# Window attention and graph experts on one core: scores by quarters of the TensorE array, shift masks accumulated by matmul

## What is computed

```python
x = x + conv(layernorm(x))          # conv: two passes of window attention
t = x.reshape(32, 1024, 128)
t = t + ffn(layernorm(t))           # graph attention -> top 2 of 4 experts

def mhsa(x, w_qkv, b_qkv, w_o, b_o, mask):      # x: (images*16, 64, 128), 8 heads of 16
    q, k, v = split(x @ w_qkv + b_qkv)
    scores = einsum('bqhd,bkhd->bhqk', q, k) / sqrt(16)
    if mask is not None:            # second pass: -1e9 where the regions differ
        scores = scores + mask[:, None, :, :]
    attn = softmax(scores)
    return einsum('bhqk,bkhd->bqhd', attn, v) @ w_o + b_o
```

## Time and profile before

| what | us |
|---|---|
| time, median of 3 runs (lowest, highest) | 8315.46 (8314.64, 8325.83) |
| the profiled execution: its time, its span | 8316.28, 8314.6 |
| TensorE busy, matmuls | 4440.4 (53%) |
| VectorE busy | 5201.6 (63%) |
| ScalarE busy | 2132.3 (26%) |
| GpSimd busy | 4861.2 (58%) |
| last subtraction of a maximum (line 1104) ends | 2250.6 |

### The profile page before, as it was taken

How to read it: one execution, slowest core, us unless ns; L and a number is a source line. 1 busy time by engine, 2 the same in 40 slices (tenths; PEclk the granted TensorE clock), 3 DMA queues, 4 the chain that set the end, 5 groups by cost and what they waited for, 6 DMA issues and landing times. The chain is left out here.

```text
span 8314.6 us, 101072 instructions
## 1 busy us (share of the span) xinstructions
PE 4440.4 (53%) x29005; PEld 2290.4 (28%) x29005; DVE 5201.6 (63%) x15789; ACT 2132.3 (26%) x3826; POOL 4861.2 (58%) x5216
## 2 busy tenths in 40 slices
PE   5889888989834445344443535445353444535200
PEld 3555555555511212122121212212121121212100
DVE  9999888988945455454545545454554545445368
ACT  4666666666510101001010100101010010101034
POOL 2221111111167777777777777777777777777573
PEclk9999999999855656556565655656565565656555
DMA  1121111111111111111111111111111111111267
GB/s 47 45 54 49 48 48 49 49 49 47 54 40 43 32 43 32 32 43 32 43 32 43 32 32 43 32 43 32 37 37 32 43 32 42 32 35 39 79 194 254
DMA packets 537622, 419.47 MB, mean 50 GB/s; under 512 B 177554, under 2 KB 450498, under 8 KB 536642
## 3 DMA queue, kind: packets, MB, share of 16 engines
q1 hardware_dynamic: 323058, 323.88, 12.0%
q0 software_dynamic: 147552, 56.96, 7.0%
q10 hardware_dynamic: 66560, 33.56, 1.4%
HBM read 203.65 MB, written 176.72 MB: 46 GB/s over the span
## 5 line engine op out<-in xcount | busy, mean ns | idle before, releaser
L1321 POOL DMA_INDIRECT edge_G<-node_rows,edge_src x4352 | 4159.5, 956 | 1326.3 <-issue 1326.3
L1358 PE MATMUL edge_cbank<-edge_ohh,edge_ohl 128*128 128x256 bf16 x4096 | 1417.4, 395 | 2951.5 <-DVE edge_ohh L1491 2878.4
L1358 PEld LDWEIGHTS edge_cbank<-edge_ohh,edge_ohl 128*128 128x128 bf16 x4096 | 427.5, 104 | 3934.8 <-DVE edge_ohh L1491 3758.9
L1491 DVE TENSOR_SCALAR edge_ohh<-edge_iob,edge_dlf 128x256 bf16<-128x256 bf16 x4096 | 1193.6, 298 | 0.0
L561 POOL TENSOR_SCALAR attn_nw<-attn_mv 128x8 f32<-128x8 f32 x64 | 89.8, 1403 | 1814.4 <-DVE attn_mv L979 1814.3
L1490 DVE TENSOR_SCALAR edge_ohl<-edge_iob,edge_dlf 128x128 bf16<-128x128 bf16 x4096 | 1084.1, 265 | 14.8 <-DVE edge_dlf L1484 14.5
L1338 ACT ACTIVATE edge_hid<-edge_hbank,edge_b1c 128x512 f32<-128x512 f32 x512 | 351.6, 687 | 2498.2 <-PE edge_hbank L1365 2498.2
L1449 DVE COPY edge_O<-edge_O 128x24 f32<-128x24 f32 x64 | 12.4, 193 | 1533.2 <-DMA edge_G<-node_rows,edge_src 1533.2
L1501 DVE TENSOR_TENSOR edge_yo<-edge_ybank,edge_b2r 128x512 f32<-128x512 f32 x256 | 176.9, 691 | 946.9 <-PE edge_ybank L1374 946.9
L1341 ACT ACTIVATE edge_w<-edge_w 128x272 f32<-128x272 f32 x64 | 27.5, 429 | 2405.3 <-DVE edge_w L1463 2405.3
L859 PE MATMUL attn_score<-attn_km,attn_qT 128*64 128x512 f32 x2048 | 537.2, 639 | 176.0 <-DMA attn_km<-attn_kT 98.0
(11 more groups left out here) (239 smaller groups left out, 6424.5 us busy)
## 6 DMA issues: line engine op xcount, KB each, us to landing
edge_G<-node_rows,edge_src POOLq DMA_INDIRECT x4352, 2.4
expert_out<-edge_yo SPq DMA_DIRECT2D x64, 1024.0 KB
comb_ye<-expert_out SPq DMA_DIRECT2D x32, 2048.0 KB, 11.8
state_rows<-edge_O SPq DMA_DIRECT2D x64, 816.0 KB, 3.7
attn_km<-attn_kT SPq DMA_DIRECT2D x2048, 16.0 KB, 1.8
attn_xin<-in_x SPq DMA_DIRECT2D x32, 512.0 KB, 4.1
attn_xres<-in_x SPq DMA_DIRECT2D x32, 512.0 KB, 5.6
x_rows<-attn_x SPq DMA_DIRECT2D x32, 512.0 KB, 3.4
```

Source lines behind the costliest of these rows:

```text
L1321: pool.indirect_dma_start(G[b][:, t, :], None, node_rows, bass.IndirectOffsetOnAxis(ap=src[b][:, t:t + 1], axis=0)).then_inc(s_g[b][2 * t ...
L1358: pe.matmul(cbank[b][:, 0:HI], ohl[:, t % RING, :], ohh[:, t % RING, :], start=(t == 0), stop=(t == HC - 1)).then_inc(s_ohp, 1)
L1491: dve.tensor_scalar(ohh[:, t % RING, :], iob[:, :], dlf[:, 1, t:t + 1], None, ALU.is_equal).then_inc(s_oh, 1)
```

## The change

1. A score matmul of 128 rows is cut into two of 64 rows (`halves`, index `a`): the first has heads 0 to 3, the second heads 4 to 7. Each has 64 rows, 64 columns and 256 moving columns, and the four of a pair of windows lie on the four quarters of the array. `score_bank` now has a bank for each half `a`, with the 256 columns of stream A and those of stream B in it, in place of a bank for each stream. `km` holds four column blocks in place of eight.
2. The mask is no longer added by VectorE. TensorE multiplies a bf16 identity (`ones`) with the bf16 mask, spread over the four heads, and accumulates it on the scores. `mask_of` now takes the window `e`: in slots 1, 3 and 5 only the right window has such matmuls (two), in slots 6 and 7 both (four).
3. `S` and `mx` follow the new order of heads and streams; the reduction, the subtraction and the exponential keep their number of elements.
4. `SLOT_US` is 8.05, and `spare` no longer counts 0.7 for a mask. The sort operations therefore fall into other slots.
5. The set-up has two operations less and a copy of the identity more, and TensorE waits for it ahead of step 2.

The diff, without the same renaming in `turn` and the views in `less_maximum`:

```diff
-SETUP = 11
+SETUP = 8
...
-        masks = sb("masks", [P, 3, WTOK])
+        masks = sb("masks", [P, 3, WTOK], BF16)
+        ones = sb("ones", [P, P], BF16)
...
-        km = [sb(f"km{s}", [P, KRING, HEADS, QWIN, WTOK]) for s in range(2)]
+        km = [sb(f"km{s}", [P, KRING, HEADS // 2, QWIN, WTOK]) for s in range(2)]
...
-        S = [sb(f"S{i}", [P, 2, HEADS, WTOK]) for i in range(RING_S)]
-        mx = sb("mx", [P, PAIRS, 2, HEADS])
+        S = [sb(f"S{i}", [P, 2, 2, HEADS // 2, WTOK]) for i in range(RING_S)]
+        mx = sb("mx", [P, PAIRS, 2, 2, HEADS // 2])
...
-        s_mask = sem("s_mask")
...
-        SLOT_US = 8.4
+        SLOT_US = 8.05
...
-            busy = (2.5 + 0.7 * (mask_of(j) is not None) if two else 1.5) + 0.8
+            busy = (2.5 if two else 1.5) + 0.8
...
-        def mask_of(j):
-            row, right = j // 2 == WGRID - 1, j % 2 == 1
-            return {(False, False): None, (False, True): 0, (True, False): 1, (True, True): 2}[(row, right)]
+        def mask_of(j, e):
+            below, right = j // 2 == WGRID - 1, j % 2 == 1 and e == 1
+            return {(False, False): None, (False, True): 0, (True, False): 1, (True, True): 2}[(below, right)]
...
-                    sp.dma_start(km[st][lo:lo + HDIM, r, head, :, :].rearrange("p w k -> p (w k)"),
+                    sp.dma_start(km[st][lo:lo + HDIM, r, head % (HEADS // 2), :, :].rearrange("p w k -> p (w k)"),
...
-                        t = S[i % RING_S][:, lo:hi, :, :].rearrange("p s h k -> p (s h k)")
+                        t = S[i % RING_S][:, :, lo:hi, :, :].rearrange("p a s h k -> p a (s h k)")
...
-                if m == 0:
-                    pe.wait_ge(s_cv, SETUP)
...
+                halves = [slice(a * P // 2, (a + 1) * P // 2) for a in range(2)]
+                out = [score_bank[e * WTOK:(e + 1) * WTOK, a, st * BANK // 2:(st + 1) * BANK // 2] for e in range(2) for a in range(2)]
+                mask = [mask_of(j, e) if s == "B" else None for e in range(2)]
                 for e in range(2):
                     w = (2 * j + e) % PAIRS
-                    last = pe.matmul(score_bank[e * WTOK:(e + 1) * WTOK, st, :], qT[st][h][:, w * WTOK:(w + 1) * WTOK],
-                                     km[st][:, q % KRING, :, (2 * j + e) % QWIN, :], start=True, stop=True)
+                    for a in range(2):
+                        last = pe.matmul(out[2 * e + a], qT[st][h][halves[a], w * WTOK:(w + 1) * WTOK],
+                                         km[st][halves[a], q % KRING, :, (2 * j + e) % QWIN, :], start=True, stop=mask[e] is None)
+                for e in range(2):
+                    if mask[e] is not None:
+                        for a in range(2):
+                            last = pe.matmul(out[2 * e + a], ones[halves[a], halves[a]],
+                                             masks[halves[a], mask[e], :].unsqueeze(1).to_broadcast([P // 2, HEADS // 2, WTOK]),
+                                             start=False, stop=True)
...
             for n in steps:
+                if n == LAG["B"]:
+                    pe.wait_ge(s_cv, SETUP)
...
-            link(dve.tensor_scalar(mi[:, 0, :], mi[:, 0, :], 6, None, ALU.logical_shift_right))
-            link(dve.tensor_tensor(mi[:, 3, :], mi[:, 3, :], mi[:, 0, :], ALU.mult))
             link(dve.tensor_tensor(mi[:, 0, :], mi[:, 2, :], mi[:, 3, :], ALU.max))
             big = NEG / SCALE
+            dve.tensor_copy(ones[:, :], ident[:, :])
...
-                if hi == 2 and mask_of(j) is not None:
-                    b = score_bank[:, 1, :].rearrange("p (h k) -> p h k", h=HEADS)
-                    dve.tensor_tensor(b, b, masks[:, mask_of(j), :].unsqueeze(1).to_broadcast([P, HEADS, WTOK]), ALU.add
-                                      ).then_inc(s_mask, 1)
-                    masked[0] += 1
-                    dve.wait_ge(s_mask, masked[0])
-                dve.tensor_reduce(top, both, AX_X, ALU.max).then_inc(s_mx, 1)
+                dve.tensor_reduce(top, scores, AX_X, ALU.max).then_inc(s_mx, 1)
```

More of the change, by code:

```diff
@@ L868, in turn @@
                     st = STREAM[s]
-                    src = S[j % RING_S][:, st, :, :].rearrange("p h k -> p (h k)")
                     for g in range(GROUPS):
-                        last = pe.transpose(turn_bank[:, st, g * P:(g + 1) * P], src[:, g * P:(g + 1) * P], ident[:, :])
+                        a, h = divmod(2 * g, HEADS // 2)
+                        src = S[j % RING_S][:, a, st, h:h + 2, :].rearrange("p h k -> p (h k)")
+                        last = pe.transpose(turn_bank[:, st, g * P:(g + 1) * P], src, ident[:, :])
                 last.then_inc(s_pt, 1)
@@ L919, in _ @@
             link(dve.tensor_tensor(mi[:, 1, :], mi[:, 0, :], mi[:, 1, :], ALU.bitwise_xor))
-            link(dve.tensor_scalar(mi[:, 2, :], mi[:, 1, :], 5, 1, ALU.logical_shift_right, ALU.bitwise_and))
+            dve.tensor_scalar(mi[:, 2, :], mi[:, 1, :], 5, 1, ALU.logical_shift_right, ALU.bitwise_and)
             link(dve.tensor_scalar(mi[:, 3, :], mi[:, 1, :], 2, 1, ALU.logical_shift_right, ALU.bitwise_and))
-            link(dve.tensor_scalar(mi[:, 0, :], mi[:, 0, :], 6, None, ALU.logical_shift_right))
-            link(dve.tensor_tensor(mi[:, 3, :], mi[:, 3, :], mi[:, 0, :], ALU.mult))
             link(dve.tensor_tensor(mi[:, 0, :], mi[:, 2, :], mi[:, 3, :], ALU.max))
             big = NEG / SCALE
+            dve.tensor_copy(ones[:, :], ident[:, :])
             dve.tensor_scalar(masks[:, 0, :], mi[:, 3, :], big, None, ALU.mult)
@@ L1083, in normalised_output @@
                                   ALU.mult).then_inc(s_nrm, 1)
-            masked = [0]
             def less_maximum(n, j):
@@ L1089, in less_maximum @@
                 lo, hi = span(n)
-                both = score_bank[:, lo:hi, :].rearrange("p s (h k) -> p (s h) k", h=HEADS)
-                rows = (hi - lo) * HEADS
-                top = mx[:, j, lo:hi, :].rearrange("p s h -> p (s h)")
+                scores = score_bank[:, :, lo * BANK // 2:hi * BANK // 2].rearrange("p a (g k) -> p a g k", k=WTOK)
+                top = mx[:, j, :, lo:hi, :].rearrange("p a s h -> p a (s h)")
                 dve.wait_ge(s_sc, k + 1)
@@ L1095, in less_maximum @@
                     dve.wait_ge(s_pt, k + 1 - RING_S)
-                if hi == 2 and mask_of(j) is not None:
-                    b = score_bank[:, 1, :].rearrange("p (h k) -> p h k", h=HEADS)
-                    dve.tensor_tensor(b, b, masks[:, mask_of(j), :].unsqueeze(1).to_broadcast([P, HEADS, WTOK]), ALU.add
-                                      ).then_inc(s_mask, 1)
-                    masked[0] += 1
-                    dve.wait_ge(s_mask, masked[0])
-                dve.tensor_reduce(top, both, AX_X, ALU.max).then_inc(s_mx, 1)
+                dve.tensor_reduce(top, scores, AX_X, ALU.max).then_inc(s_mx, 1)
                 dve.wait_ge(s_mx, k + 1)
-                dve.tensor_tensor(S[j % RING_S][:, lo:hi, :, :].rearrange("p s h k -> p (s h) k"), both,
-                                  top.unsqueeze(2).to_broadcast([P, rows, WTOK]), ALU.subtract).then_inc(s_sub, 1)
+                dve.tensor_tensor(S[j % RING_S][:, :, lo:hi, :, :].rearrange("p a s h k -> p a (s h) k"), scores,
+                                  top.unsqueeze(3).to_broadcast([P, 2, (hi - lo) * HEADS // 2, WTOK]), ALU.subtract).then_inc(s_sub, 1)
             for n in steps:
```

## The result

| run | us, median (lowest to highest) | ratio to the kernel before, 95% interval |
|---|---|---|
| before | 8320.08 (8314.64 to 8325.83) | |
| changed | 8223.25 (8221.01 to 8232.19) | 0.9889 [0.9876, 0.9901] |

The change saves 97 us by the medians (92 by the ratio); 158 were forecast. All of it is in the attention stage: the last subtraction of a maximum ends at 2158.8 us instead of 2250.6, 91.8 earlier, and the spans of the two profiled executions differ by 91.3.

A forecast was written before the change was run, and what follows sets the result against it. Long two-stream steps were bound by a TensorE, ScalarE and SyncE loop, short ones by VectorE. Gains of 136 us inside and 27 outside made 163, less 5 for the clock: 158, so 8158 us, range 8090 to 8230.

The forecast's parts named there:

- The loop of TensorE, ScalarE and SyncE: Two-stream steps: these engines work one after another for 71.56 us, setting a long step of 70.9 us.
- the upper 30 us: Top of the range, some 30 us beyond 8201, for masks on TensorE at their upper price.
- the sum per step: Two-stream steps: 13 long ones gain 5.0 us each, 17 short ones 4.2, together 136 us.
- the long steps: Thirteen of 30 two-stream steps, 68 us or more, set by something else than VectorE's work; each to fall 5.0 us.
- I take 5 us off for all steps: Slot 4: TensorE's wait drops the clock to 0.50, slowing the half group behind; 5 us taken from the 163 gained.
- The slots behind the residual: Slots 6 and 7: whole score groups save 0.86 us each, less masks; slot 7 to next slot 0 falls 0.66.
- waits stay: Rival: idle time returns in slot 4 and at slot 6's residual, only VectorE's 115 us count: 8201, chance 0.25.
- set by VectorE's work: Seventeen short two-stream steps: VectorE's work sets them; each gains between its net 3.0 and 5.0 us, taken as 4.2.
- Outside the two-stream steps: Outside the 30 two-stream steps: 7 us of masks and 20 of sort operations leave VectorE, 27 us gained.
- SyncE's series: km transfers into slot 4: 13.03 us from first issue to stream B's scores, forecast to stay as it is.
- The row halves: Rival: row halves of score groups do not run side by side, a group takes 3.66 us: about 8610, chance 0.05.
- its rival: Rival: granted clock in two-stream steps sinks to 0.85, costing 150 us in all: 8303, chance 0.05.

The follow-up runs named there:

- e9: Scores in quarters, masks left on VectorE, quarter 2's key transfers first in SyncE's order, against the kernel before: 8186.27 us, ratio 0.9823.
- e1: Changed kernel with quarter 2's key transfers moved ahead of the loads of x and xres in SyncE's order: 8079.85 us, ratio 0.9705 to the kernel before.
- e2: Kernel before with only quarter 2's key transfers moved ahead of the loads of x and xres in SyncE's order: 8210.79 us, ratio 0.9864.
- e3: Kernel before with masks on TensorE, scores still 128 rows by 512 columns, sort operations placed as in the changed kernel: 8329.48 us, ratio 1.0003.
- e6: Changed kernel with eight overwritten filler matmuls ahead of stream B's wait for km in slot 4: 8172.82 us, ratio 0.9811 to the kernel before.
- e7: e1 with transposes CZ0 and CZ1 ahead of stream B's projections in slot 6: 8105.64 us, ratio 0.9745 to the kernel before.
- e5: Changed kernel with SLOT_US 8.4 and the 0.7 us for masks in spare, as before: 8236.26 us, ratio 0.9883 to the kernel before.
- e4: Kernel before with scores in quarters, masks still added by VectorE, sort operations placed as before: 8248.12 us, ratio 0.9906.

## Why the prediction was right and where it was not

**Right.** The direction, and that the time would come from attention alone. The size of a score group: 1.08 forecast, 1.09 measured. By the Trainium skill's page "TensorE: Matmul & The Clock Gate" (Measured speedup vs the span model) it would have been 1.19 (estimate); the measurement lies nearer to full overlap of four quarters. The masks on TensorE: from the group's start to the transposes 1.02 us without (1181.96 to 1182.98), 1.13 with four (1217.53 to 1218.66), so 0.11; forecast 0.11 for two and 0.2 for four. The mask's price on VectorE: 98 us where VectorE is the bound (e9 to e1), 115 forecast. The loop of TensorE, ScalarE and SyncE as what sets the steps: e1, e2 and e3 show it. The time itself, 8223, lies in the range, 7 us from its upper end. That it does so is partly luck: the upper 30 us were meant for dearer masks on TensorE, which did not come, and were filled by the failures listed next.

**Wrong: the sum per step.** I gave 5.0 us to the long steps and 4.2 to the short ones; measured from slot 0's scores to the next it was 3.7 (69.2 to 65.5) and 1.9 (65.3 to 63.3). Over all 30 it was 66.9 to 64.3, 2.6 a step, 78 us in place of 136. Three steps failed inside, and a fourth sum outside.

1. *"I take 5 us off for all steps" for the clock.* This is the mis-sized term. The segment behind the wait in slot 4 should have fallen by 0.43 and grew by 0.74: 1.17 a step, 35 us. Of this 0.85 us, some 25 us in all, is the clock, by the runs with the filler; time on the half clock in this segment rose from 4.20 to 6.21 us. The other 0.31 is work: the planner has put transposes of sort keys behind stream B's scores in 14 of the 26 steps, 9 before, at 1.59 us each (e6). I had written that a faster TensorE waits there as long or longer, and had the row with 1.98 for 1.08 us, but took only 0.17 us a step for it. In step 18 the low clock lasts over slot 4's transposes, products and projections as well. e6 shows that 50 us of the changed kernel's time hang on the clock.
2. *The slots behind the residual.* From slot 7 to slot 0 nothing was gained, 0.65 a step or 20 us. In the profile after, TensorE's transposes of slot 7 (L793) wait for VectorE's output (34.8 us in all; the same wait of the kernel before is 16.3 in its trace), which stands behind the residual, for which VectorE waits 45.1 us instead of 28.6. The rival "waits stay" had named this place. No run takes this wait away by itself; e7 replaced it by another. Not all of the 0.65 is this wait: in e5, with the old tables, the segment falls to 7.17. How much is wait and how much moved work stays open.
3. *The short steps "set by VectorE's work".* e3 takes 3.6 us a step off VectorE, and the short steps grow by 1.1 us; e4 leaves VectorE's work as it was, and they fall by 2.0. Less work on VectorE only made its wait longer (154 to 274 us in e3).

4. *Outside the two-stream steps.* 27 us were forecast and 13.6 came: step 2 starts 3.8 us earlier (142.7 to 138.9), and the part behind step 31, up to the last subtraction, takes 91.5 us in place of 101.3. VectorE's busy time in these two parts fell by 4.9 and 11.4 us only. Whether the 3.8 come from the sort operations taken out there or from the shorter memsets of km, which I had put at nothing (GpSimd's first work on the statistics starts at 12.36 in place of 15.79), is not settled, nor why not more came.

**The rivals.** "VectorE's waits stay" (8201) was nearest to the time: they grew from 154 to 176 us. But its sum, VectorE's 115 us for the masks, came close by luck: the masks alone bring nothing (e3), and most of the gain comes from the quarters (e4). Its reason, that SyncE's series does not shrink, was the right one, and the profile had it; I took the mean loop to shorten by more than the series and the clock allow. The series also grew by 0.48 a step, 14 us, where I had written that it stays as it is; why the transfers were issued a little slower (10.09 to 10.55 us for 15 of them) stays open. The row halves ran together, and the clock did not sink as far as its rival had it (0.93).

## What to carry to other kernels

An engine that is busy 90% of a stage need not be its bound: take the loop apart into segments between engines and queues, and price an edit only where it lies on that loop. The same edit was worth nothing, 14, 51 or 98 us here, depending on what else had been done, and a reorder of one transfer queue that saves no work was worth more (1.4%) than either half of the change. Where TensorE waited for a transfer here, the price was the wait and the matmuls behind it that ran on the lower clock, so a shorter matmul ahead of a fixed wait can give part of its gain back.

## What the runs showed of the hardware that I had not expected

- After an idle stretch of 4.42 us TensorE ran for some eight of the next ten microseconds on its 1.2 GHz level, while it was busy (granted clock 0.59); with 3.72 us of filler in that gap the transposes behind took 1.10 us and not 1.97. How long it stayed low varied: in e3's step 18, behind 4.20 us of idle, the transposes took 1.62 us and the products were back at 1.13 (granted clock 0.81 from 1261.0 to 1269.2).
- Four quarters of 64 x 64 with float32 operands overlapped fully: 16 records of 256 columns in 1.09 us, where two column halves took 1.94 us for 8 records of 512.
- A bf16 matmul that accumulates on float32 scores in the same quarters costs some 0.11 us for two or four of them; as one or two matmuls of 512 columns on the full rows (e3) it costs 0.21 to 0.22 us (from the scores' start to the transposes 1.87 us without, 2.08 and 2.09 with).
